# Key reads of an attention kernel shared by two issuing engines: lower partition quarters from SP, upper quarters from ACT

## The chip, the cores and the metric

The kernel runs on one core of one Trainium2 chip. The metric is the time of one execution on the device in microseconds (us). A core has a matrix engine (PE), three engines for elementwise work (DVE, ACT, POOL) and SP, which here only issues transfers. 16 DMA engines move data between device memory and the on-chip memory, which has 128 partitions.

## What is computed

Three layers over 8 sequences of 64 rows by 512, with a context of 8 x 1601 x 512, all in f32. Cut to what matters:

```python
def _L0_xattn_ref(q, k, v, Wq, bq, Wk, bk, Wv, bv):
    qp = q @ Wq + bq;  kp = k @ Wk + bk;  vp = v @ Wv + bv
    attn = softmax(qp @ kp.T / sqrt(512))
    return attn @ vp
...
x = x + _L0_xattn_ref(_layernorm(x), ctx_1024, ctx_1024, ...)
x = x + _L0_attn_ref(_layernorm(x), ...)      # 16 heads, sigmoid gates, no softmax
x = x + _L0_ffn_ref(_layernorm(x), ...)       # each row to one of 8 experts
return x
```

## The kernel before

The 8 sequences are worked in four pairs (p = 0 to 3; k = 0, 1 is the member of a pair). Pair 0 is written out, pairs 1 and 2 are the two passes of a loop, pair 3 is written out again, and the experts follow. The key projection is folded into the queries, so the scores are products of queries with the raw context rows. For that the rows are wanted twice: as they are (CTX, for the weighted sums) and turned (CT, for the scores).

**Two ways to turn.** The 1601 keys are 13 tiles of 128, two tiles to a group (groups 0 to 6). In some groups PE turns the tiles of CTX and ACT (k = 0) and DVE (k = 1) copy them into CT (`turn_keys`, `move_keys`). The others are "split" groups (1, 2, 3 in pair 0; 1 to 5 later): `load_split` reads them a second time from device memory straight into FF, in four partition quarters of 32 (`quad`), each quarter taking 128 of the 512 columns in runs of 512 bytes, and DVE turns them in 32x32 blocks by two STREAM_TRANSPOSE (`turn_split`, L847), no PE needed. A part of `SPLIT_PARTS` is what one wait covers: (1, 2), (3), (4), (5). Each part takes 8 transfers (4 quarters x 2 members): 256 KB each for the part of two groups, 128 KB each for one group. Only when all 8 have landed may DVE start on a group of the part. FF has three slots for groups, so 4 and 5 reuse those of 1 and 2, and a part may be read once the group that held its slot has been turned (semaphore `keysT_made`).

**Order of the work.** Every engine works through its own program in order. In a pair p, PE runs 14 half groups of scores (u = 0 to 13); between them stand the steps of the second layer for pair p-1 (L1169 to L1376). Then the scores' softmax is made (DVE maxima, ACT exponentials L686), PE turns the numerators (L1261), ACT and DVE move them (L347), and PE makes the weighted sums with CTX (L1290) in four chunks c = 0 to 3. Here ACT also makes 16 small copies of the next pair's queries (L678), and DVE, at c = 1, turns the next pair's groups 1 and 2. Behind these four transposes DVE has the last numerators (c = 3), the routing steps L975 to L995 of pair p-1 and the reciprocal of the softmax sums (L895). ACT's L693 needs this reciprocal, and PE's first transposes of the next pair's second-layer steps (L1169, A<-sq) need L693.

**Who issues.** SP issues all reads of the context: in `next_split` the next pair's part 1 (group 3) and part 0 (groups 1 and 2), in `load_pair` CTX chunks 0 and 1, then parts 2 and 3 (groups 4 and 5) and CTX chunks 3 and 2. ACT issues none. In pair 0's prologue SP issues parts 0 and 1 while PE and ACT make the queries (ACT L661, L667).

Of the kernel before, what the change touches and what calls it, by code (L numbers as in the profile page):

```python
# [8 lines left out]
P = 128  # L9
# [8 lines left out]
QUADS = P // Q  # L18
BLOCKS = GT * P // Q
SLOT_OF = {1: 0, 2: 1, 3: 2, 4: 0, 5: 1}  # L20
SPLIT_PARTS = ((1, 2), (3,), (4,), (5,))
EARLY = 2
TURN_FIRST = 6
CHUNKS = [(0, 4), (4, 8), (8, FULL), (FULL, KT)]
NCH = len(CHUNKS)

# [89 lines left out]
def program(nc, A):  # L116
# [4 lines left out]
    with ctx:  # L121
# [181 lines left out]
        def settle(eng):  # L303

            eng.sem_inc(s["passed"], 1)
# [17 lines left out]
        def split_turned(p, n):  # L323

            return 2 * n if is_first(p) else 2 * len(NEXT.split) * p + 2 * (len(FIRST.split) - len(NEXT.split) + n)
# [5 lines left out]
        def move_keys(eng, copy, p, k, t):  # L331

            if t is None:
                return
            o = order_of(p)
            pos, w = o.at[t // GT], P if t < FULL else TAIL
            eng.wait_ge(s[f"turned{k}"], keys_moved(p, o.tiles.index(t) + 1))

            slot_free(eng, p, pos)
            copy(ctxT[:, pos % 2, k, :, (t % GT) * P:(t % GT) * P + w], turned_bank(TR[k])[:, :, 0:w]).then_inc(s[f"moved{k}"], 1)  # L340

        def move_numerators(eng, copy, p, c):

            lo, hi = CHUNKS[c]
            w = P if c < NCH - 1 else TAIL
            eng.wait_ge(s[f"turned{c % 2}"], numerators_moved(p, c // 2 + 1))
            copy(probs[0:w, lo:hi, :], TR[c % 2][0:w, 0:(hi - lo) * P].rearrange("p (t q) -> p t q", q=P)).then_inc(s[f"moved{c % 2}"], 1)  # L347

        @block.sync  # L350
        def _(sp):
            def load_ctx(b, k, c):
# [8 lines left out]
            def load_split(p, part):

                first, slot = SPLIT_PARTS[part][0] * GT * P, SLOT_OF[SPLIT_PARTS[part][0]]
                n = len(SPLIT_PARTS[part]) * BLOCKS
                for quad in range(QUADS):
                    for k in range(2):
                        src = A["ctx"][bass.ds(2 * p + k, 1), first:first + n * Q, quad * P:(quad + 1) * P]
                        sp.dma_start(split[quad * Q:(quad + 1) * Q, k, slot * BLOCKS:slot * BLOCKS + n, :],
                                     src.rearrange("a (b r) d -> r (a b) d", r=Q)).then_inc(s_split[part], 16)

            def next_split(p):

                if is_first(p):
                    sp.wait_ge(s["keysT_made"], split_turned(0, 2))
                    load_split(1, 0)
                    sp.wait_ge(s["keysT_made"], split_turned(0, 3))
                    load_split(1, 1)
                    return
                sp.wait_ge(s["keysT_made"], split_turned(p, order_of(p).split.index(3) + 1))
                settle(sp)  # L380
                load_split(p + 1, 1)
                sp.wait_ge(s["keysT_made"], split_turned(p, len(order_of(p).split)))
                settle(sp)
                load_split(p + 1, 0)

            def load_chunk(p, c):

# [6 lines left out]
            def load_pair(p):  # L394

                load_chunk(p, 0)
                load_chunk(p, 1)
                sp.wait_ge(s["keysT_made"], split_turned(p, 2))
                settle(sp)
                load_split(p, 2)  # L400
                load_split(p, 3)
                load_chunk(p, 3)
                load_chunk(p, 2)

# [22 lines left out]
            load_x(0)  # L427
            for c in (0, 2, 3):
                load_chunk(0, c)
            load_split(0, 0)  # L430
            load_split(0, 1)

            sp.wait_ge(s["qp_made"], 2 * DC)
            load_weight(awq, "awq", "aq_in")
# [205 lines left out]
        def _(act):  # L640
# [9 lines left out]
            for half in range(2):  # L650
                if half == 0:
                    move_x0(0)
                    move_x0(1)
                    act.wait_ge(s["vec_in"], 16)

                for m in range(DC):
                    if half == 0 and m == DC - 1:
                        move_x0(2)
                        move_x0(3)
                    act.wait_ge(s["qp_made"], DC * half + m + 1)  # L660
                    a.activation(qpT[:, m, 2 * P * half:2 * P * (half + 1)], AB[m % 2][:, 0:2 * P], ACT.Identity,  # L661
                                 bias=vec[:, 0, m:m + 1]).then_inc(s["qp_moved"], 1)

            def move_qk(first, m):
                n = slice(0, P) if first else slice(P, PAIRS * P)
                act.wait_ge(s["qk_made"], (m if first else DC + m) + 1)
                a.copy(qk[:, m, n], AB[m % 2][:, n]).then_inc(s["qk_moved"], 1)  # L667

            for m in range(DC):
                move_qk(True, m)  # L670

            def next_queries(p, last, chunks=range(DC)):

                act.wait_ge(s["qk_moved"], 2 * DC)
                act.wait_ge(s["scored"], GROUPS * (p - 1) + last)
                for m in chunks:
                    for j in range(QUADS):
                        a.copy(qcurP[m * Q:(m + 1) * Q, j, :], qk[j * Q:(j + 1) * Q, m, bass.ds(p * P, P)]).then_inc(s["qcurP_made"], 1)  # L678
# [10 lines left out]
            def attention(p, step):  # L689
# [49 lines left out]
                elif step == "route":  # L739
                    act.wait_ge(s["top_made"], p + 1)  # L740
                    act.wait_ge(s["pow3"], p + 1)
                    a.activation(sm[:, 2:3], sm[:, 0:1], ACT.Exp, scale=rstd[:, 3:4]).then_inc(s["en_made"], 1)

            for t in FIRST.tiles[:GT]:
                move_keys(act, a.copy, 0, 0, t)
            move_qk(False, 0)
            move_qk(False, 1)
            for t in FIRST.tiles[GT:]:
                move_keys(act, a.copy, 0, 0, t)
            act.wait_ge(s["c_made"], 1)  # L750
            a.copy(call[:], AB[1][:, 0:PAIRS + E]).then_inc(s["c_moved"], 1)
            exponentials(0)
# [796 lines left out]
```

## Time and profile before

| | |
|---|---|
| median of 3 runs | 333.71 us (331.84 to 335.01) |
| the profiled execution | 333.99 us, of which the span of the trace is 332.3 us |
| PE busy | 301.6 us (91%) |
| DVE, ACT, POOL busy | 161.2, 90.7, 78.4 us |
| TensorE's granted clock, mean | 0.996 of full speed |
| moved by the 16 DMA engines | 74.27 MB, 224 GB/s over the span |
| reads of FF from the context | 80 of 128 KB and 32 of 256 KB, all issued by SP |

The page of the profile gives shares; the views of the trace give single waits and times. In a timeline a row is the start, the length, the engine, the line of the kernel and the operation with its tiles (written<-read), and in square brackets how long the engine stood idle before it and what ended that. SPq and ACTq are the instruction streams (sequencers) of SP and ACT: a DMA_DIRECT2D there is the issue of a transfer, not the transfer.

### The profile page before, as it was taken

How to read it: one execution, taken by the hardware profiler on the slowest of the kernel's cores; microseconds unless marked ns; L12 is line 12 of the kernel's file. 1: busy time of each engine (PE TensorE's matmuls, PEld its weight loads, DVE VectorE, ACT ScalarE, POOL GpSimd, SP SyncE). 2: the span in 40 equal slices, each digit the busy share in tenths (PEclk: the TensorE clock that was granted, in tenths of full speed). 3: DMA queues.
4: the chain of work that ended last, by engine and by line, in shares of the span. 5: the costliest groups of instructions: out<-in, count | busy, mean ns of one | idle time of the engine just before them, and what ended most of it. 6: DMA issues, size and time to landing. Idle time of an engine off the chain costs nothing. (4 is left out here: it accounts for less than half of the span.)

```text
span 332.3 us, 5209 instructions
## 1 busy us (share of the span) xinstructions
PE 301.6 (91%) x1806; PEld 159.8 (48%) x1806; DVE 161.2 (49%) x364; ACT 90.7 (27%) x209; POOL 78.4 (24%) x84
## 2 busy tenths in 40 slices
PE   0999899999899889999989999999998989899792
PEld 0788567643454544445455445455543344443330
DVE  3303338537263763828185833738561354735431
ACT  1132230235112346321234442124411013411110
POOL 5000003167022500112340020135102246103202
PEclk9999999999999999999999999999999999999998
DMA  7999999999999998999949699952715996153300
GB/s 250 390 374 172 184 311 387 211 187 257 387 211 228 279 187 132 375 250 227 324 77 192 116 393 220 258 204 83 298 63 145 396 411 266 28 205 109 119 2 34
DMA packets 61364, 74.27 MB, mean 224 GB/s; under 512 B 3187, under 2 KB 40083, under 8 KB 60320
## 3 DMA queue, kind: packets, MB, share of 16 engines
q1 hardware_dynamic: 59792, 69.23, 80.2%
q0 software_dynamic: 1552, 4.78, 4.0%
q8 instruction: 12, 0.20, 0.3%
q14 instruction: 8, 0.07, 0.1%
HBM read 70.85 MB, written 3.67 MB: 224 GB/s over the span
## 5 line engine op out<-in xcount | busy, mean ns | idle before, releaser
L1251 PE MATMUL SC<-CT_sb,QC_sb 128*64 128x256 f32 x384 | 50.4, 389 | 0.3 <-DVE CT_sb L847 0.2
L847 DVE STREAM_TRANSPOSE CT_sb<-FF_sb 128x1024 f32<-128x1024 f32 x36 | 42.4, 1220 | 14.3 <-DMA FF_sb<-ctx 12.7
L1290 PE MATMUL ST<-CTX_sb,PR_sb 128*64 128x512 f32 (+1 forms) x208 | 48.2, 600 | 1.1 <-ACT PR_sb L347 1.1
L1251 PEld LDWEIGHTS SC<-CT_sb,QC_sb 128*64 128x64 f32 x384 | 24.7, 136 | 17.2 <-issue 9.0
L1176 PE MATMUL A<-AW_sb,normT_sb 128*128 128x512 f32 x64 | 29.4, 599 | 1.3 <-DVE normT_sb L918 1.3
L1290 PEld LDWEIGHTS ST<-CTX_sb,PR_sb 128*64 128x64 f32 (+1 forms) x208 | 13.9, 136 | 23.2 <-issue 22.3
L532 POOL TENSOR_TENSOR rn_sb<-ss_sb,nhalf_sb 128x16 f32<-128x16 f32 x4 | 11.7, 2915 | 33.9 <-DVE ss_sb L923 33.9
L1176 PEld LDWEIGHTS A<-AW_sb,normT_sb 128*128 128x128 f32 x64 | 11.7, 190 | 14.8 <-issue 12.2
L1169 PE MATMUL TR<-ident_sb,CTX_sb 128*128 128x128 f32 (+1 forms) x128 | 16.1, 266 | 2.3 <-DVE CT_sb L340 1.1
L1196 PE MATMUL A<-AW_sb,WQK_sb 128*128 128x256 f32 x64 | 16.4, 422 | 0.8 <-ACT AW_sb L645 0.8
L1169 PEld LDWEIGHTS TR<-ident_sb,CTX_sb 128*128 128x128 f32 (+1 forms) x128 | 12.9, 141 | 8.7 <-issue 5.6
L340 DVE COPY CT_sb<-TR 128x512 f32<-128x512 f32 (+1 forms) x16 | 10.0, 625 | 13.2 <-PE TR L1169 13.0
L340 ACT COPY CT_sb<-TR 128x512 f32<-128x512 f32 (+1 forms) x16 | 8.6, 535 | 25.6 <-PE TR L1169 25.5
L1176 PE MATMUL A<-AO_sb,rawT_sb 128*128 128x512 f32 x32 | 14.8, 605 | 0.7 <-DVE rawT_sb L962 0.6
L1176 PE MATMUL A<-WV_sb,rawT_sb 128*128 128x512 f32 x32 | 14.8, 605 | 0.7 <-ACT rawT_sb L696 0.7
L1196 PEld LDWEIGHTS A<-AW_sb,WQK_sb 128*128 128x128 f32 x64 | 13.6, 215 | 3.3 <-issue 1.1
L1219 PE MATMUL A<-AO_sb,WQK_sb 128*128 128x128 f32 (+1 forms) x64 | 14.6, 383 | 0.7 <-ACT AO_sb L661 0.7
L678 ACT COPY QC_sb<-QK_sb 32x128 f32 (+1 forms) x48 | 14.2, 295 | 1.1
L900 DVE TENSOR_TENSOR x_sb<-A,xrow_sb 128x512 f32<-128x512 f32 x4 | 2.8, 692 | 23.0 <-PE A L1176 23.0
L535 POOL TENSOR_TENSOR rn_sb<-ss_sb,nhalf_sb 128x16 f32<-128x16 f32 x4 | 11.6, 2903 | 7.5 <-DVE ss_sb L930 7.5
L855 DVE COPY QC_sb<-QK_sb 32x128 f32<-32x128 f32 x16 | 3.9, 241 | 18.5 <-ACT QK_sb L667 18.0
L526 POOL TENSOR_TENSOR rstd_sb<-rstd_sb,halves_sb 128x3 f32<-128x3 f32 x4 | 3.5, 872 | 38.3 <-DVE rstd_sb L908 38.3
(227 smaller groups left out, 459.0 us busy)
## 6 DMA issues: line engine op xcount, KB each, us to landing
CTX_sb<-ctx SPq DMA_DIRECT2D x24, 1024.0 KB, 10.7
FF_sb<-ctx SPq DMA_DIRECT2D x80, 128.0 KB, 7.2
FF_sb<-ctx SPq DMA_DIRECT2D x32, 256.0 KB, 7.9
CTX_sb<-wgu SPq DMA_DIRECT2D x4, 1024.0 KB, 9.4
CTX_sb<-wdn SPq DMA_DIRECT2D x5, 512.0 KB, 12.8
FF_sb<-wgu SPq DMA_DIRECT2D x2, 1024.0 KB, 6.6
rows<-XR_sb SPq DMA_DIRECT2D x3, 512.0 KB, 10.7
CTX_sb<-ctx SPq DMA_DIRECT2D x8, 130.0 KB
```

Source lines behind the costliest of these rows:

```text
L340: copy(ctxT[:, pos % 2, k, :, (t % GT) * P:(t % GT) * P + w], turned_bank(TR[k])[:, :, 0:w]).then_inc(s[f"moved{k}"], 1)
L532: g.tensor_tensor(rn[:, 0:HEADS], ss[:, 0:HEADS], nhalf[:, 0:HEADS], ALU.pow).then_inc(s["powq"], 1)
L535: g.tensor_tensor(rn[:, HEADS:], ss[:, HEADS:], nhalf[:, HEADS:], ALU.pow).then_inc(s["powk"], 1)
L678: a.copy(qcurP[m * Q:(m + 1) * Q, j, :], qk[j * Q:(j + 1) * Q, m, bass.ds(p * P, P)]).then_inc(s["qcurP_made"], 1)
L847: v.transpose(ctxT[:, pos % 2, k, :, :].rearrange("p c (b r) -> p b c r", r=Q), split[:, k, at:at + BLOCKS, :].rearrange("p b (c r) -> p b ...
L855: v.tensor_copy(qcurP[m * Q:(m + 1) * Q, j, :], qk[j * Q:(j + 1) * Q, m, 0:P]).then_inc(s["qcurP_made"], 1)
L1169: last = t_.transpose(bank[:, c * w:c * w + n], rows[:, c * P:(c + 1) * P], ident[0:n, 0:n])
L1176: last = t_.matmul(bank, left[:, c, :], right[:, c, :], start=(c == 0), stop=(c == DC - 1))
L1196: last = t_.matmul(AB[m % 2][:, 0:2 * P], wq[:, c, m * P:(m + 1) * P], xnT[:, c, 2 * P * half:2 * P * (half + 1)], start=(c == 0), stop=(c ...
L1219: last = t_.matmul(AB[m % 2][:, n], wkT[:, c, m * P:(m + 1) * P], qpT[:, c, n], start=(c == 0), stop=(c == DC - 1))
L1251: last = t_.matmul(out[q, :], (qcurP if split_group else qcur)[:, c, q], ctxT[:, pos % 2, k, c, 0:n], start=(c == 0), stop=(c == DC - 1))
L1290: last = t_.matmul(ST[q, :], probs[0:w, t, q], ctxb[0:w, k, t, :], start=(t == 0), stop=(t == KT - 1))
```

## The change

`load_split` becomes a helper with an engine and a list of quarters. SP keeps the quarters 0 and 1 (partitions 0 to 63, `LOWER`, 4 transfers a part), ACT gets the quarters 2 and 3 (`UPPER`). Groups 4 and 5 become one part of 8 transfers of 256 KB (before: two parts, 16 of 128 KB). Over the kernel 112 transfers, all from SP, become 88, 44 from each. ACT's issues stand in its program at these places: in the prologue one after each of the last four L661 and one after each of the first four L667; in pair 0 after its last key copy and after the first numerators; in pairs 1 to 3 part 2 after u = 1; in pairs 1 and 2 the next pair's part 1 after u = 5 and part 0 after the first numerators.

```diff
-SPLIT_PARTS = ((1, 2), (3,), (4,), (5,))
+SPLIT_PARTS = ((1, 2), (3,), (4, 5))
+LOWER, UPPER = ([(quad, k) for quad in range(lo, lo + QUADS // 2) for k in range(2)] for lo in (0, QUADS // 2))
+UPPER_REST, UPPER_FIRST = 1, 5
...
+        def load_split(eng, p, part, quads):
...
+            for quad, k in quads:
+                src = A["ctx"][bass.ds(2 * p + k, 1), first:first + n * Q, quad * P:(quad + 1) * P]
+                eng.dma_start(split[quad * Q:(quad + 1) * Q, k, slot * BLOCKS:slot * BLOCKS + n, :],
...
-                load_split(p, 2)
-                load_split(p, 3)
+                load_split(sp, p, 2, LOWER)
...
+                    if half == 1:
+                        load_split(act, 0, 0, UPPER[m:m + 1])
...
                 move_qk(True, m)
+                load_split(act, 0, 1, UPPER[m:m + 1])
...
+            def upper_first(p, n, part):
+                act.wait_ge(s["keysT_made"], split_turned(p, n))
...
+                load_split(act, p + 1, part, UPPER)
+            def upper_rest(p):
+                act.wait_ge(s["keysT_made"], split_turned(p, 2))
...
                     move_keys(act, a.copy, p, 0, NEXT.tile(u))
+                    if u == UPPER_REST:
+                        upper_rest(p)
+                    if u == UPPER_FIRST and not is_last(p):
+                        upper_first(p, NEXT.split.index(3) + 1, 1)
                 exponentials(p)
                 for step in by_max:
                     attention(p - 1, step)
                 move_numerators(act, a.copy, p, 0)
+                if not is_last(p):
+                    upper_first(p, len(NEXT.split), 0)
```

ACT's program in the loop, from the softmax's exponentials (PR<-SC) on, before. An ISA or REGISTER_ALU row is register work for the instruction behind it.

```order
L686 ACTIVATE PR_sb,esum_sb<-SC,mx_sb 128x512 x2
L686 ACTIVATE PR_sb,esum_sb<-ST,mx_sb 128x65
L346 REGISTER_ALU
L347 COPY PR_sb<-TR 128x512 [waits turned0]
L675 REGISTER_ALU [waits qk_moved]
L678 ISA [waits scored]
L678 COPY QC_sb<-QK_sb 32x128
```

The same place of the changed kernel (its L349 is L347 of before):

```order
L690 ACTIVATE PR_sb,esum_sb<-SC,mx_sb 128x512 x2
L690 ACTIVATE PR_sb,esum_sb<-ST,mx_sb 128x65
L348 REGISTER_ALU
L349 COPY PR_sb<-TR 128x512 [waits turned0]
L750 REGISTER_ALU
L358 ISA [waits keysT_made]
L358 DMA FF_sb<-ctx 32x16x128
L358 ISA
L358 DMA FF_sb<-ctx 32x16x128
L358 ISA
L358 DMA FF_sb<-ctx 32x16x128
```

Four issues for the next pair's groups 1 and 2 now stand between the numerators' copy and the query copies.

ACT's program in pair 0's prologue, where it moves the projected queries out of PSUM (AO<-A, then QK<-A), before:

```order
L661 ACTIVATE AO_sb<-A,vec_sb 128x256 [waits qp_made] x2
L645 COPY AW_sb<-TR 128x4x128 [waits xnT_turned] x2
L661 ACTIVATE AO_sb<-A,vec_sb 128x256 [waits qp_made] x5
L667 COPY QK_sb<-A 128x128 [waits qk_made] x4
L340 COPY CT_sb<-TR 128x4x128 [waits turned0] x2
```

and changed:

```order
L662 ACTIVATE AO_sb<-A,vec_sb 128x256 [waits qp_made]
L358 DMA FF_sb<-ctx 32x16x128
L662 ACTIVATE AO_sb<-A,vec_sb 128x256 [waits qp_made]
L358 DMA FF_sb<-ctx 32x16x128
L670 COPY QK_sb<-A 128x128 [waits qk_made]
L358 DMA FF_sb<-ctx 32x8x128
L670 COPY QK_sb<-A 128x128 [waits qk_made]
L358 DMA FF_sb<-ctx 32x8x128
```

Behind each of eight moves there is now an issue that stands ahead of the next move.

SP's program from the reads of pair 1's groups 1 and 2 (32x16x128) and group 3 (32x8x128) to pair 1's first CTX chunk, before:

```order
L368 DMA FF_sb<-ctx 32x16x128 [waits keysT_made]
L368 DMA FF_sb<-ctx 32x16x128 x7
L368 DMA FF_sb<-ctx 32x8x128 [waits keysT_made]
L368 DMA FF_sb<-ctx 32x8x128 x7
L406 DMA AO_sb<-awo 128x4x512 [waits c_made,qk_made]
L356 DMA CTX_sb<-ctx 128x4x512 [waits pv_chunk]
```

and changed:

```order
L358 DMA FF_sb<-ctx 32x16x128 [waits keysT_made]
L358 DMA FF_sb<-ctx 32x16x128 x3
L358 DMA FF_sb<-ctx 32x8x128 [waits keysT_made]
L358 DMA FF_sb<-ctx 32x8x128 x3
L407 DMA AO_sb<-awo 128x4x512 [waits c_made,qk_made]
L368 DMA CTX_sb<-ctx 128x4x512 [waits pv_chunk]
```

SP comes to the CTX chunk after 8 issues in place of 16.

## Rows read from the trace of the kernel before

**Rows 1.** The page, busy time, share of the span and instructions.
```profile
PE 301.6 (91%) x1806; PEld 159.8 (48%) x1806; DVE 161.2 (49%) x364; ACT 90.7 (27%) x209; POOL 78.4 (24%) x84
```

**Rows 2.** Waits: who waited for whom, us in total, times, longest.
```profile
PE TR L1169 <- DMA CTX_sb<-ctx: 1.0, 1, 1.0
DVE CT_sb L847 <- DMA FF_sb<-ctx: 12.7, 4, 5.4
```

**Rows 3.** Stretches of pair 1 and pair 2: length, busy per engine, clock, DMA, GB/s.
```profile
81.80:140.60 58.80, 54.83 (x335) 27.90 (x331) 31.76 (x67) 19.24 (x46) 10.04 (x8) 1.00 1.06 259
140.60:197.70 57.10, 54.68 (x335) 28.08 (x335) 32.43 (x69) 19.23 (x46) 11.97 (x11) 1.00 0.98 222
```

**Rows 4.** Timeline of PE: start, length, work, idle before and its end.
```profile
89.45 0.66 PE L1169 MATMUL TR<-ident_sb,CTX_sb 128*128 128x128 f32 x4 [0.95 <-DMA CTX_sb<-ctx]
...
117.88 0.63 PE L1169 MATMUL A<-ident_sb,kh_sb 128*128 128x128 f32 x4 [1.14 <-DVE res_sb L945]
...
142.03 0.66 PE L1169 MATMUL A<-ident_sb,sq_sb 128*128 128x128 f32 x4 [0.39 <-ACT sq_sb L693]
...
198.72 0.66 PE L1169 MATMUL A<-ident_sb,sq_sb 128*128 128x128 f32 x4
```

**Rows 5.** Timeline of DVE, the block transposes that stood waiting in pairs 1 and 2.
```profile
102.45 2.37 DVE L847 STREAM_TRANSPOSE CT_sb<-FF_sb 128x1024 f32<-128x1024 f32 x2 [5.40 <-DMA FF_sb<-ctx]
...
132.43 4.63 DVE L847 STREAM_TRANSPOSE CT_sb<-FF_sb 128x1024 f32<-128x1024 f32 x4 [4.31 <-DMA FF_sb<-ctx]
...
186.38 4.63 DVE L847 STREAM_TRANSPOSE CT_sb<-FF_sb 128x1024 f32<-128x1024 f32 x4 [1.17 <-DMA FF_sb<-ctx]
```

**Rows 6.** Timeline of ACT around the places where issues are put.
```profile
28.10 0.47 ACT L661 ACTIVATE AO_sb<-A,vec_sb 128x256 f32<-128x256 f32 x1 [1.25 <-PE A L1196]
...
30.78 0.27 ACT L667 COPY QK_sb<-A 128x128 f32<-128x128 f32 x1 [0.63 <-PE A L1219]
...
88.61 0.59 ACT L340 COPY CT_sb<-TR 128x512 f32<-128x512 f32 x1 [4.57 <-PE TR L1169]
...
125.88 0.59 ACT L347 COPY PR_sb<-TR 128x512 f32<-128x512 f32 x1 [0.20 <-PE TR L1261]
126.37 2.54 ACT L678 COPY QC_sb<-QK_sb 32x128 f32 x8
131.43 0.59 ACT L738 COPY normT_sb<-A 128x512 f32<-128x512 f32 x1 [2.53 <-PE A L1169]
...
137.90 2.53 ACT L678 COPY QC_sb<-QK_sb 32x128 f32 x8
...
182.98 0.59 ACT L347 COPY PR_sb<-TR 128x512 f32<-128x512 f32 x1 [0.20 <-PE TR L1261]
```

**Rows 7.** Timeline of SP's issues.
```profile
16.90 22.03 SPq L368 DMA_DIRECT2D FF_sb<-ctx  x16
...
75.63 1.15 SPq L356 DMA_DIRECT2D CTX_sb<-ctx  x1
...
130.61 0.38 SPq L356 DMA_DIRECT2D CTX_sb<-ctx  x1
...
172.94 6.09 SPq L368 DMA_DIRECT2D FF_sb<-ctx  x8
...
187.71 0.96 SPq L356 DMA_DIRECT2D CTX_sb<-ctx  x2
```

**Rows 8.** Line L368 in 172 to 180 us: issue in ns, min/median/max.
```profile
L368 SPq DMA_DIRECT2D FF_sb<-ctx x8: 316/348/1477, 172.9 to 177.8; - x8
```

**Rows 9.** Stretches with FF reads alone, then CTX reads alone; columns as rows 3.
```profile
178.00:182.00 4.00, 3.80 (x24) 1.99 (x25) 2.04 (x6) 1.63 (x5) 0.00 (x0) 1.00 1.25 184
...
190.00:194.00 4.00, 4.00 (x25) 1.83 (x23) 2.03 (x6) 0.36 (x2) 0.00 (x0) 1.00 1.04 400
```

**Rows 10.** DMA in 114 to 122 us, 40 slices of 0.2 us, FF reads.
```profile
GB/s 151 164 172 179 177 184 177 161 197 200 197 169 192 202 220 151 141 159 164 225 220 228 207 151 167 166 179 264 228 197 143 146 282 202 187 192 154 143 141 164
```

**Rows 11.** Line L776, the end of ACT's loop, in 138 to 140 us.
```profile
L776 ACTq COMPARE_BRANCH  x1: 45/45/45, 138.9 to 138.9; - x1
```

More of the change, by code:

```diff
@@ L347, in move_numerators @@
             copy(probs[0:w, lo:hi, :], TR[c % 2][0:w, 0:(hi - lo) * P].rearrange("p (t q) -> p t q", q=P)).then_inc(s[f"moved{c % 2}"], 1)
+        def load_split(eng, p, part, quads):
+            first, slot = SPLIT_PARTS[part][0] * GT * P, SLOT_OF[SPLIT_PARTS[part][0]]
+            n = len(SPLIT_PARTS[part]) * BLOCKS
+            for quad, k in quads:
+                src = A["ctx"][bass.ds(2 * p + k, 1), first:first + n * Q, quad * P:(quad + 1) * P]
+                eng.dma_start(split[quad * Q:(quad + 1) * Q, k, slot * BLOCKS:slot * BLOCKS + n, :],
+                              src.rearrange("a (b r) d -> r (a b) d", r=Q)).then_inc(s_split[part], 16)
         @block.sync
@@ L359, in load_ctx @@
                     sp.dma_start(ctxb[0:TAIL, k, FULL, :], src).then_inc(s_ctx[k][c], 16)
[L361 to L369, printed above, removed]
             def next_split(p):
@@ L374, in next_split @@
                     sp.wait_ge(s["keysT_made"], split_turned(0, 2))
-                    load_split(1, 0)
+                    load_split(sp, 1, 0, LOWER)
                     sp.wait_ge(s["keysT_made"], split_turned(0, 3))
-                    load_split(1, 1)
+                    load_split(sp, 1, 1, LOWER)
                     return
@@ L380, in next_split @@
                 settle(sp)
-                load_split(p + 1, 1)
+                load_split(sp, p + 1, 1, LOWER)
                 sp.wait_ge(s["keysT_made"], split_turned(p, len(order_of(p).split)))
                 settle(sp)
-                load_split(p + 1, 0)
+                load_split(sp, p + 1, 0, LOWER)
             def load_chunk(p, c):
@@ L429, in _ @@
                 load_chunk(0, c)
-            load_split(0, 0)
-            load_split(0, 1)
+            load_split(sp, 0, 0, LOWER)
+            load_split(sp, 0, 1, LOWER)
             sp.wait_ge(s["qp_made"], 2 * DC)
@@ L742, in attention @@
                     a.activation(sm[:, 2:3], sm[:, 0:1], ACT.Exp, scale=rstd[:, 3:4]).then_inc(s["en_made"], 1)
+            def upper_first(p, n, part):
+                act.wait_ge(s["keysT_made"], split_turned(p, n))
+                if not isinstance(p, int):
+                    settle(act)
+                load_split(act, p + 1, part, UPPER)
+            def upper_rest(p):
+                act.wait_ge(s["keysT_made"], split_turned(p, 2))
+                settle(act)
+                load_split(act, p, 2, UPPER)
             for t in FIRST.tiles[:GT]:
@@ L749, in _ @@
                 move_keys(act, a.copy, 0, 0, t)
+            upper_first(0, 2, 0)
             act.wait_ge(s["c_made"], 1)
@@ L756, in _ @@
                 move_numerators(act, a.copy, 0, c)
+                if c == 0:
+                    upper_first(0, 3, 1)
             next_queries(1, FIRST.at[FIRST.split[-1]] + 1)
```

## The prediction

> **What bounds the kernel now.** I read the page first: PE is busy for 91% of the span, no other engine for half of it [rows 1]. The clock is full, so PE's own work sets the time, and a change of reads can only move what PE stands idle for. Next the waits: only one wait of PE names a transfer, 1.0 us. DVE waited 12.7 us in four times for the split reads in FF [rows 2], so the question is how much of DVE's lateness comes through to PE. For that I set pairs 1 and 2 side by side, since both are passes of the same loop. Pair 1 took 58.80 us, pair 2 57.10, with the same 335 matmuls and nearly the same PE busy time [rows 3]. The surplus of 1.7 us is what late reads cost PE. The timeline shows where. At 89.45 PE waits 0.95 us for a CTX chunk. At 117.88 it waits 1.14 us for a DVE product that was late because DVE had waited 5.40 us for group 4 at 102.45 [rows 4, 5]; to this I put the other 0.75 us of the surplus. The rest of the waits for FF reached PE hardly at all. So a perfect supply of reads is worth 1.7 us, plus 0.39 us at 142.03 (below). That is 0.6% of the time, and no faster transfer can give more while PE has its work to do.
>
> **The gain.** SP has 8 issues fewer ahead of pair 1's first CTX chunk, which it sent at 75.63 [rows 7]. At 0.35 us each [rows 8] these are 2.8 us, so the wait of 0.95 us goes. For the other 0.75 us group 4 must land by about 101.5 in place of 102.45. It now comes in one part with group 5, 2 MB where DVE waited for 1 MB, sent by both engines from about 83. Eight such reads took 13.4 us in pair 2 (below), and the tail of four CTX chunks is ahead of them: 97 to 101. I take the whole 1.7 us, and 0.95 as the lower bound.
>
> **ACT's issues, where they cost nothing.** An issue of 256 KB into a queue with room took SP 316 to 348 ns (median), up to 1477 once the queue was full [rows 8]. With the register work of the loop in between I count 0.55 us each on ACT, 2.2 us for four, 0.35 to 0.5 us each in the unrolled prologue. In the prologue ACT stands idle 1.25 us before each L661 and 0.63 us before each L667 [rows 6], which covers the eight issues. After u = 1 there are 4.57 us free before 88.61. After the first numerators, the query copies end 2.2 us later, at 131.1 in place of 128.9, and the next move, at 131.43, is not touched [rows 6]. Uncovered, the 44 issues at 0.5 us would be 22 us, so the cover matters (second rival).
>
> **The loss.** This is what the order of ACT shows. Groups 1 and 2 of the next pair are a part that DVE needs whole. SP still sends its half as soon as group 5 is turned (in pair 2 at 172.94 [rows 7]). ACT sends the other half only behind the exponentials and the first numerators. In pair 2 that is 10 us behind SP's half.
>
> How long does this half take? In pair 2 of before, eight reads (2.10 MB) sent from 172.94 [rows 7] had landed when DVE started at 186.38 [rows 5]: 13.4 us. At the 184 GB/s that FF reads reach [rows 9] the data take 11.4 us, so 2.0 us are the way in and out. Four reads (1.05 MB) then take 5.7 + 2.0 = 7.7 us, alone in the engines. They land at 133.7 and 190.8. But SP sends CTX chunks at 130.61 and 187.71 [rows 7], which meet the last 1.1 us or so of the data. Shared evenly this adds 1.1 us (134.8, 191.9), and if CTX gets two turns of three, 2.2 us (135.9, 193.0). I take the middle of the first two, 134.3 and 191.4, since nothing shows how two queues share.
>
> When must they be there? In pair 1 DVE started at 132.43, and PE's step 9.6 us later at 142.03 already waited 0.39 us for the chain behind it (four transposes 4.63 us, numerators, routing, reciprocal, L693) [rows 4, 5]. So there is no slack: the loss is 134.3 - 132.43 = 1.9 us (1.3 to 3.5). In pair 2 the same step began at 198.72 without a wait. 9.6 us ahead of it is 189.1, which DVE's 186.38 met with 2.7 us to spare. The loss is 191.4 - 189.1 = 2.3 us (1.7 to 3.9). Pair 0's reads for pair 1 go from both engines at 57 us and are early. Parts 1 and (4, 5) have many microseconds left in every pair, and after pair 3's scores nothing is changed.
>
> A rule of the Trainium skill bears on the rate: *SBUF — State Buffer*, section "Door 1: The DMA port swizzle", says that partitions 0 to 63 reach only 8 of 16 ports and 64 to 127 the other 8, with 196 GB/s measured for 64 partitions. The trace agrees: 184 GB/s for quarters against 400 for all partitions [rows 9]. Its next section says that two transfers to the two halves do not add up. Slices of 264 and 282 GB/s stand where the reads go from quarter to quarter [rows 10], which speaks for some adding up. By either the late half lands alone, so the sum stays.
>
> **Sum.** -1.7 + 1.9 + 2.3 = +2.5 us on the profiled execution of 333.99 us, 336.5. The median of the runs shown lies 0.3 us below that execution: **336.2 us**, 0.7% above the median of before. With the bounds of the two losses (3.0 to 7.4) and a gain from 0.95 to 1.7 it is 335.0 to 340.2.
>
> **Rivals.**
> *The late half does no harm (0.20).* If four reads, alone, run well above 184 GB/s or the copies' sequencer lets them go earlier, both losses shrink. At 400 GB/s [rows 9] they take 2.6 + 2.0 us and land at 130.6 and 187.7, ahead of 132.43 and 189.1. Only the gain is left, and at best the 0.39 us with it: 331.6 to 332.0. For it: the peaks [rows 10]. Against: 184 GB/s was held over 4 us [rows 9].
> *ACT's issues are held up by SP's (0.27).* In the prologue, with its queue full, SP took 22.03 us for 16 issues, 1.4 us each [rows 7]. If ACT must wait while SP's issue is stuck, its issue costs 1.4 us more. Each of four moves then comes 1.4 + 0.5 - 1.25 = 0.6 us late, and of four more 1.4 + 0.35 - 0.63 = 1.1 us, with PE waiting for each of them: up to 6.8 us, half of it if SP is through early. After u = 1 in pair 1, where SP's queue is full again, four issues take 8 us against 4.57 [rows 6], 3 us more. This decides from 1.3 us an issue on, and gives 336.2 + 3 to 10 = 339 to 346, about 342. Against it: ACT's queue itself is empty.
> *Perfetto Trace Analysis* in the Trainium skill, section "DMA Instruction — HWDGE (DVE, Sync)", says that the descriptor generator is locked for one issue at a time; no run here shows a second issuing engine, so it is this rival's rule and not the forecast's.
> *It is faster by over 1% (0.04).* It needs 3.3 us and PE's waits for reads hold 2.1. It would take some other stall that transfers cause inside busy time, and pairs 1 and 2 have the same busy time at 259 and 222 GB/s [rows 3].
>
> **How the numbers follow.** The forecast has 0.47, its own range 335.0 to 339.0. The rest, 0.02, is for what I don't see. About 1% is what a measurement of this kernel can tell from no change: below 330.4 is faster, above 337.0 slower. Of the forecast's 0.47 I put a quarter above 337.0, and all of the second rival: 0.12 + 0.27 = 0.39 slower. Faster 0.05, the same 0.56. The range for 8 in 10 goes from 331.8 to 342.0: it leaves out the upper half of the second rival and the lowest edge of the first.
>
> **What would show it.** Right: in pairs 1 and 2 DVE's transposes of the next pair's groups 1 and 2 wait longer for FF (start near 134 and 191, counted as above), PE waits for L693 about 2 us in each, PE no longer waits at a CTX turn in pair 1, and ACT's issues take 0.3 to 0.5 us. The pairs would take about 57.1 + 1.9 and 57.1 + 2.3, with the wait at the end of one counted in the next. Wrong: ACT's issues of over a microsecond and PE waiting for L661 and L667 in the first 35 us (second rival), or DVE starting at its old times (first). Group 4 landing later than 103 in pair 1 would make the gain's second half wrong.

## The result and the profile after

The changed kernel takes 347.62 us (median of 4 runs, 345.06 to 349.03) against 332.92 us for the kernel before (4 runs, 331.84 to 335.01): a ratio of 1.042, 95% interval 1.034 to 1.051. It is 14.7 us slower. The forecast was 336.2 us, range 331.8 to 342.0, with 0.39 for slower. The forecast lies 11.4 us too low, and the time is outside the range. Ratios, here and below, leave out the few executions in a slower state of the chip.

The profiled execution took 345.06 us with a span of 343.3 us, 11.0 us more than before. First the page, busy time and then the granted clock in 40 slices:

```profile
PE 304.0 (89%) x1806; PEld 160.5 (47%) x1806; DVE 162.2 (47%) x364; ACT 91.0 (26%) x209; POOL 78.7 (23%) x84
...
PEclk9999999999999999699999999999999999999998
```

PE does the same 1806 matmuls [rows 1]. Its busy time grew by 2.4 us, and one slice shows a lower clock; the other 8.6 us are idle. This execution is the fastest of the four. The other three, with mean clocks of 0.968 to 0.981 against its 0.987, took 1.9 to 4.0 us longer, so the 14.7 us between the medians hold more of a low clock than this trace shows. Who waits for whom, us in total, times and longest:

```profile
DVE CT_sb L873 <- DMA FF_sb<-ctx: 32.8, 5, 8.1
...
PE A L1195 <- DVE res_sb L971: 3.2, 3, 1.1
PE A L1366 <- issue: 2.4, 2, 1.2
PE A L1397 <- DVE onehot_sb L1008: 2.1, 2, 1.7
PE A L1195 <- DVE qh_sb L952: 2.0, 2, 1.4
```

DVE's waits for the split reads went from 12.7 to 32.8 us [rows 2], and PE now waits for DVE's products in several places. The timeline of DVE tells which reads are late, start, length, work and the idle time before it:

```profile
99.98 2.37 DVE L873 STREAM_TRANSPOSE CT_sb<-FF_sb 128x1024 f32<-128x1024 f32 x2 [5.15 <-DMA FF_sb<-ctx]
132.77 4.62 DVE L873 STREAM_TRANSPOSE CT_sb<-FF_sb 128x1024 f32<-128x1024 f32 x4 [7.12 <-DMA FF_sb<-ctx]
164.48 2.37 DVE L873 STREAM_TRANSPOSE CT_sb<-FF_sb 128x1024 f32<-128x1024 f32 x2 [6.68 <-DMA FF_sb<-ctx]
195.86 4.62 DVE L873 STREAM_TRANSPOSE CT_sb<-FF_sb 128x1024 f32<-128x1024 f32 x4 [5.72 <-DMA FF_sb<-ctx]
227.31 2.37 DVE L873 STREAM_TRANSPOSE CT_sb<-FF_sb 128x1024 f32<-128x1024 f32 x2 [8.11 <-DMA FF_sb<-ctx]
```

A row x2 is group 4, a row x4 the next pair's groups 1 and 2. Before, group 4 was waited for in pair 1 alone [rows 5]. Now it is late in pairs 2 and 3 too, which the forecast did not have.

Where the 11.0 us arise is read from PE, the same work in both kernels. From the timeline of before, four rows beside those of [rows 4]:

```profile
82.76 0.66 PE L1169 MATMUL A<-ident_sb,sq_sb 128*128 128x128 f32 x4
...
149.15 1.09 PE L1169 MATMUL TR<-ident_sb,CTX_sb 128*128 128x128 f32 x8
...
196.78 1.08 PE L1290 MATMUL ST<-CTX_sb,PR_sb 65*64 65x512 f32 x4
...
234.52 0.69 PE L1251 MATMUL ST<-CT_sb,QC_sb 128*64 128x65 f32 x16
```

and after:

```profile
81.72 0.66 PE L1195 MATMUL A<-ident_sb,sq_sb 128*128 128x128 f32 x4
...
115.42 0.63 PE L1195 MATMUL A<-ident_sb,kh_sb 128*128 128x128 f32 x4 [0.96 <-DVE res_sb L971]
...
138.87 0.18 PE L1397 MATMUL A<-onehot_sb,before_sb 128*128 128x8 f16 x1 [1.74 <-DVE onehot_sb L1008]
...
140.90 1.98 PE L1277 MATMUL SC<-CT_sb,QC_sb 128*64 128x256 f32 x8 [0.81 <-ACT QC_sb L682]
142.81 1.12 PE L1195 MATMUL A<-ident_sb,sq_sb 128*128 128x128 f32 x4
...
151.81 1.09 PE L1195 MATMUL TR<-ident_sb,CTX_sb 128*128 128x128 f32 x8
...
202.10 1.08 PE L1316 MATMUL ST<-CTX_sb,PR_sb 65*64 65x512 f32 x4
...
206.12 0.66 PE L1195 MATMUL A<-ident_sb,sq_sb 128*128 128x128 f32 x4 [1.08 <-ACT sq_sb L697]
...
245.59 0.69 PE L1277 MATMUL ST<-CT_sb,QC_sb 128*64 128x65 f32 x16
```

| the same work, before and after | offset | arose since the last row |
|---|---|---|
| 82.76, 81.72 (pair 1's first layer-2 step) | -1.0 | -1.0: not by the change, see below |
| 117.88, 115.42 (pair 1, middle) | -2.5 | -1.4: the gain |
| 142.03, 142.81 (pair 2's first layer-2 step) | +0.8 | +3.2: groups 1 and 2 late |
| 149.15, 151.81 | +2.7 | +1.9: the clock |
| 196.78, 202.10 (end of pair 2's sums) | +5.3 | +2.7: group 4 late in pair 2 |
| 198.72, 206.12 | +7.4 | +2.1: groups 1 and 2 late |
| 234.52, 245.59 (end of pair 3's scores) | +11.1 | +3.7: group 4 late in pair 3 |

So groups 1 and 2 cost 3.2 + 1.9 + 2.1 = 7.2 us, groups 4 and 5 cost 6.4 us, and 2.5 us came back. The first 1.0 us of these stood already in the prologue, ahead of ACT's first issue at 21.97, as the same move of ACT shows, before and after:

```profile
21.20 0.47 ACT L661 ACTIVATE AO_sb<-A,vec_sb 128x256 f32<-128x256 f32 x1 [1.09 <-PE A L1196]
...
20.23 0.47 ACT L662 ACTIVATE AO_sb<-A,vec_sb 128x256 f32<-128x256 f32 x1 [1.09 <-PE A L1222]
```

From trace to trace of the later experiments too PE comes to pair 1 at different times, 81.7 to 84.3 where the clock stays full, so pairs are compared below by their own lengths.

The clock is seen in the stretches (length, busy time of PE, PEld, DVE, ACT, POOL, granted clock, DMA share, GB/s):

```profile
139.00:145.00 6.00, 5.19 (x24) 2.47 (x24) 1.80 (x8) 2.92 (x8) 2.36 (x4) 0.59 1.15 279
145.00:155.00 10.00, 10.00 (x54) 5.29 (x52) 4.22 (x11) 1.17 (x2) 1.33 (x2) 0.91 1.15 228
```

A mean of 0.59 lies near the lower of TensorE's two levels, 1.2 GHz. Behind the waits of 1.74 and 0.81 us, eight score products take 1.98 us where 1.08 is usual.

### Why group 4 is late

SP's issues before, from the reads of groups 4 and 5 in pair 2 to CTX chunks 3 and 2:

```profile
137.29 13.31 SPq L368 DMA_DIRECT2D FF_sb<-ctx  x16
151.31 0.85 SPq L359 DMA_DIRECT2D CTX_sb<-ctx  x2
```

after, SP and then ACT:

```profile
140.07 1.24 SPq L358 DMA_DIRECT2D FF_sb<-ctx  x1
141.63 2.87 SPq L371 DMA_DIRECT2D CTX_sb<-ctx  x2
144.74 0.97 SPq L368 DMA_DIRECT2D CTX_sb<-ctx  x2
...
144.27 2.07 ACTq L358 DMA_DIRECT2D FF_sb<-ctx  x4
```

Before, the CTX chunks stood behind the split reads in one queue, and the first of them was issued at 151.31, behind the last read. Now SP is done with its half by 141.3 and sends the chunks, while ACT's half goes out from 144.27 in a queue of its own. The DMA queues in 150 to 156 us of after, packets, MB, share of 16 engines (q1 is SP's, q10 ACT's):

```profile
q1 hardware_dynamic: 678, 1.35, 82.4%
q10 hardware_dynamic: 666, 0.33, 26.9%
```

Before, the eight reads issued in 137 to 144 us had 7.3/8.1/8.4.

The Trainium skill, *DMA: Bandwidth & Descriptors*, section "Queues, rings and completion order", says that each engine takes turns between queues packet by packet. The trace agrees: 678 against 666.

### The profile page after: what moved, and what is told of

Read it like the earlier page. It is cut to its first block and busy times, and to the rows that moved or that the text cites. A ratio compares the mean times of both kernels' runs of the same rounds, so it can differ in the third digit from the quotient of the medians.

```text
span 343.3 us, 5166 instructions
## 1 busy us (share of the span) xinstructions
PE 304.0 (89%) x1806; PEld 160.5 (47%) x1806; DVE 162.2 (47%) x364; ACT 91.0 (26%) x209; POOL 78.7 (23%) x84
## 5 line engine op out<-in xcount | busy, mean ns | idle before, releaser
L873 DVE STREAM_TRANSPOSE CT_sb<-FF_sb 128x1024 f32<-128x1024 f32 x36 | 42.4, 1220 | 34.4 <-DMA FF_sb<-ctx 32.8
L1277 PE MATMUL SC<-CT_sb,QC_sb 128*64 128x256 f32 x384 | 52.3, 400 | 1.8 <-ACT QC_sb L682 0.8
L1222 PE MATMUL A<-AW_sb,WQK_sb 128*128 128x256 f32 x64 | 15.7, 409 | 0.8 <-ACT AW_sb L646 0.8
L1245 PE MATMUL A<-AO_sb,WQK_sb 128*128 128x128 f32 (+1 forms) x64 | 14.6, 384 | 0.7 <-ACT AO_sb L662 0.7
L1222 PEld LDWEIGHTS A<-AW_sb,WQK_sb 128*128 128x128 f32 x64 | 13.1, 208 | 3.1 <-issue 1.1
## 6 DMA issues: line engine op xcount, KB each, us to landing
CTX_sb<-wdn SPq DMA_DIRECT2D x5, 512.0 KB, 12.8
```

What stands on the lines that cost most here:

```text
L873: v.transpose(ctxT[:, pos % 2, k, :, :].rearrange("p c (b r) -> p b c r", r=Q), split[:, k, at:at + BLOCKS, :].rearrange("p b (c r) -> p b ...
L1222: last = t_.matmul(AB[m % 2][:, 0:2 * P], wq[:, c, m * P:(m + 1) * P], xnT[:, c, 2 * P * half:2 * P * (half + 1)], start=(c == 0), stop=(c ...
L1245: last = t_.matmul(AB[m % 2][:, n], wkT[:, c, m * P:(m + 1) * P], qpT[:, c, n], start=(c == 0), stop=(c == DC - 1))
L1277: last = t_.matmul(out[q, :], (qcurP if split_group else qcur)[:, c, q], ctxT[:, pos % 2, k, c, 0:n], start=(c == 0), stop=(c == DC - 1))
```

## The experiments

Two theories from the traces. **Place:** ACT's halves of groups 1 and 2 go out behind exponentials and numerators, 8 to 10 us after SP's halves. **Sharing:** the halves of groups 4 and 5 lie beside the CTX chunks in place of ahead of them. Rivals: a second queue costs as such; ACT's issues are held up by SP's; the merge of groups 4 and 5 costs by itself. All times are medians, ratios against the kernel before on the same chip. "Less" below is against the changed kernel's 347.62 us, which was measured apart from these runs. The kernel before had medians of 332.92, 333.41, 333.39 and 333.92 us in the four groups of measurements, so a difference of 1 us between groups says nothing.

| kernel | edit against | us | ratio, 95% |
|---|---|---|---|
| a_rest_sp | changed: part (4, 5) all from SP | 340.81 | 1.018 to 1.029 |
| b_first_sp | changed: groups 1, 2 of pairs 2, 3 all from SP | 340.77 | 1.019 to 1.034 |
| c_both_sp | changed: a and b | 334.54 | 0.999 to 1.007 |
| e_held | changed: CTX chunks held back | 340.87 | 1.017 to 1.028 |
| f_early | changed: ACT's issues for 1, 2 earlier | 340.32 | 1.017 to 1.030 |
| i_early_held | changed: e and f | 332.03 | 0.993 to 0.9998 |
| g_early_rest_sp | changed: f and a | 333.70 | 0.997 to 1.003 |
| h_unmerged | changed: groups 4, 5 as two parts | 340.49 | 1.008 to 1.024 |
| k_unmerged_early_held | changed: e, f and h | 333.16 | 0.996 to 1.001 |
| d_merge | before: groups 4, 5 as one part | 339.54 | 1.015 to 1.026 |
| j_fill | changed: PE kept busy in a wait | 347.45 | 1.038 to 1.050 |

### Taking one half back to SP

```diff
-                load_split(sp, p, 2, LOWER)
+                load_split(sp, p, 2, LOWER + UPPER)
...
-                    if u == UPPER_REST:
-                        upper_rest(p)
```

> The changed kernel, but SP issues all eight reads of groups 4 and 5 again (still one part); ACT keeps the upper halves of the other parts. Theory Q (queue sharing): in the changed kernel ACT's half of groups 4 and 5 takes turns, packet by packet, with the 2 MB of the CTX chunk that SP sent ahead of it or beside it, lands 7 to 8 us later than DVE wants it, and PE loses 2.7 us in pair 2 and 3.7 us in pair 3, plus some of the time at a lower clock. Then this run gains 6 to 9 us on the changed kernel: 339 to 341, and DVE's transposes of group 4 stand no longer than in the kernel before. Rival U (a second issuing engine as such costs, by whatever way): 12 of 44 issues fewer give 12/44 of 14.7 us, so 343 to 344. Rival M (one part for groups 4 and 5 is the cause): no gain, 347.

340.81 us, 6.8 less, as expected. DVE waits for group 4 in pair 1 alone (5.45 us), and for groups 1 and 2 as in the changed kernel (7.12 and 6.05 us).

```diff
-                load_split(sp, p + 1, 0, LOWER)
+                load_split(sp, p + 1, 0, LOWER + UPPER)
...
-                if not is_last(p):
-                    upper_first(p, len(NEXT.split), 0)
```

> The changed kernel, but for pairs 2 and 3 SP issues all eight reads of groups 1 and 2; ACT keeps the rest. Theory P (place in ACT's program): ACT sends its half only behind the first numerators, 8 to 10 us after SP; it costs PE 2.8 us in pair 1 and 2.4 us in pair 2, and the idle time ahead of the dip of the granted clock around 139 us. Then this run gains 5 to 8 us: 339.5 to 342.5, and the clock has no dip there. Rival U: 8 of 44 issues fewer, 345. Rival M: 347.

340.77 us, 6.85 less, as expected. The waits for groups 1 and 2 go to 1.59 and 1.42 us, those for group 4 stay (9.30 and 7.70 us in pairs 2 and 3), and the clock stays at 1.00 from 130 to 150 us.

> Both of the former: ACT issues only for pair 0, for pair 1's groups 1 to 3 and the upper halves of group 3. Theories P and Q together: no late reads are left, the early CTX chunk of pair 1 stays, 331.5 to 333. Rival U: 24 of 44 issues are left on ACT, so half of the loss, 340. Rival M: 347, or at least well above 335.

Both edits: 334.54 us, 13.1 less. The two losses add up, and are 7 us each by the medians (what of this is the clock is said below). The 331.5 to 333 that was expected is missed by 1.5 us. ACT still issues 24 reads here (pair 0's, pair 1's groups 1 and 2, and group 3's), and the time is 0.3% above the kernel before, not told from none, so a second issuing engine as such costs 2 us at most (the interval ends at 1.007).

### Mending the order and leaving the issues on ACT

```diff
                 load_split(sp, p, 2, LOWER)
+                sp.wait_ge(s_split[2], 16 * 2 * QUADS * p)
+                settle(sp)
                 load_chunk(p, 3)
```

> The changed kernel with one wait more: SP sends the CTX chunks 3 and 2 only when the eight reads of groups 4 and 5 have landed. ACT's issues, their places and the merged part are as in the changed kernel. Theory Q: ACT's half has the engines to itself and SP's half, lands within 8 us of its issue, so group 4 is in time: 339 to 341 as with these reads on SP. Rival U and rival M: 347 or slower, since a wait is added and nothing taken away.

340.87 us, 6.75 less, with every one of the 44 issues still on ACT. Only the time at which SP sends the CTX chunks (and what stands behind them in its program) changed, so without the sharing group 4 is not late. Whether the sharing alone makes it late is asked below. DVE's wait for it in pair 1 is 1.38 us.

```diff
+                if not is_last(p):
+                    upper_first(p, len(NEXT.split), 0)
                 exponentials(p)
                 for step in by_max:
                     attention(p - 1, step)
                 move_numerators(act, a.copy, p, 0)
-                if not is_last(p):
-                    upper_first(p, len(NEXT.split), 0)
```

> The changed kernel with ACT's four issues for the next pair's groups 1 and 2 moved ahead of its exponentials (all groups have been turned by then, and ACT stands idle there 3.9 us). Nothing else moves, the number of issues and of queues stays. Theory P (the place in ACT's program makes the half late): DVE finds groups 1 and 2 landed or nearly so, PE's 1.7 us wait for the one-hot rows in pair 1 and the clock's dip behind it go: 339.5 to 342.5, as with these reads on SP, and groups 4 still late. Rival U (the second queue as such): 347.

340.32 us, 7.3 less. The waits for groups 1 and 2 are 1.57 and 1.31 us: the place in ACT's program was the cause.

> Both mends at once, all 44 issues still on ACT: groups 1 and 2 sent ahead of the exponentials, CTX chunks 3 and 2 held until groups 4 and 5 have landed. Theories P and Q together: no read is late, and pair 1's CTX wait stays away: 331.5 to 334, at best 0.4% below the kernel before. Rival U: clearly above 335.

Both: **332.03 us** (10 runs, 331.02 to 333.95), 15.6 less than the changed kernel and 0.4% below the kernel before; the interval, 0.993 to 0.9998, only just leaves out no change. Its DVE timeline:

```profile
96.98 2.37 DVE L875 STREAM_TRANSPOSE CT_sb<-FF_sb 128x1024 f32<-128x1024 f32 x2 [1.23 <-DMA FF_sb<-ctx]
127.55 4.62 DVE L875 STREAM_TRANSPOSE CT_sb<-FF_sb 128x1024 f32<-128x1024 f32 x4 [1.73 <-DMA FF_sb<-ctx]
155.98 2.37 DVE L875 STREAM_TRANSPOSE CT_sb<-FF_sb 128x1024 f32<-128x1024 f32 x2 [3.14 <-DMA FF_sb<-ctx]
184.17 4.62 DVE L875 STREAM_TRANSPOSE CT_sb<-FF_sb 128x1024 f32<-128x1024 f32 x4 [1.26 <-DMA FF_sb<-ctx]
210.51 2.37 DVE L875 STREAM_TRANSPOSE CT_sb<-FF_sb 128x1024 f32<-128x1024 f32 x2 [1.01 <-DMA FF_sb<-ctx]
```

Of that hardly anything reaches PE: the 0.41 us at 139.73 below was 0.39 us before. Pairs 1 and 2 in its timeline of PE:

```profile
82.64 0.66 PE L1197 MATMUL A<-ident_sb,sq_sb 128*128 128x128 f32 x4
...
139.73 0.66 PE L1197 MATMUL A<-ident_sb,sq_sb 128*128 128x128 f32 x4 [0.41 <-ACT sq_sb L699]
...
196.41 0.66 PE L1197 MATMUL A<-ident_sb,sq_sb 128*128 128x128 f32 x4
```

Pair 1 takes 57.1 us where it was 59.3 (82.76 above to 142.03 [rows 4]), pair 2 takes 56.7 as before.

> The changed kernel with ACT's issues for groups 1 and 2 ahead of the exponentials and the merged part (4, 5) all from SP. Theory (place in ACT's program, queue sharing): both losses go, since the halves of groups 1 and 2 are sent in time and the CTX chunks stand behind the part (4, 5) in one queue again. It should come to the kernel that has both all on SP (334.5 us): 333 to 336 us, with DVE waiting for FF at most about 5 us in pair 1 (group 4, behind a full queue). If a second queue as such costs something: 338 us or more.

333.70 us, the time of the kernel before (333.92 on that chip). DVE waits 5.01 us for group 4 in pair 1, yet pair 1 takes 57.7 us (84.28 to 141.97), 1.6 us less than before. The gain is there, and is lost ahead of it: PE comes to pair 1 1.5 us later than before, 0.6 us of it already ahead of ACT's first issue and 0.9 us by ACT's issues in the prologue (see "ACT's issues" below).

### The merge of groups 4 and 5

```diff
-SPLIT_PARTS = ((1, 2), (3,), (4, 5))
+SPLIT_PARTS = ((1, 2), (3,), (4,), (5,))
...
                 load_split(sp, p, 2, LOWER)
+                load_split(sp, p, 3, LOWER)
...
                 load_split(act, p, 2, UPPER)
+                load_split(act, p, 3, UPPER)
```

> The changed kernel with groups 4 and 5 as two parts again, each split between SP and ACT (8 issues of 128 KB on either engine after u = 1). It tells how much of the lateness of groups 4 and 5 (about 6.4 us of the 14.7 us lost) comes from DVE having to wait for both groups at once, and how much from ACT's half sharing the DMA engines packet for packet with SP's CTX chunks. If it is the merge: group 4's upper half is half the data, lands some 5 us sooner than the 14.4 us of the changed kernel, DVE does not wait for it, and the time is 341 to 343 us. If it is the sharing: group 4 is better but group 5 is as late as before, the time is 344 to 347 us. If eight issues in a row hold up ACT's key copies: over 347 us.

340.49 us, 7.1 less, 0.5 us below the 341 to 343 that was expected if the merge matters. No wait of DVE for group 4 or 5 is left in its trace: two waits, 12.8 us, both for groups 1 and 2. So it takes both, the sharing and the merge, to make group 4 late in pairs 2 and 3: with the merge but the chunks behind the reads again (a_rest_sp, e_held) it is in time, and with the sharing but without the merge it is too. Either edit removes the same 7 us, so the 7 us can't be divided between them.

> The changed kernel with all three mended: ACT's issues for groups 1 and 2 ahead of the exponentials, SP waiting for the FF reads of groups 4 and 5 before it sends CTX chunks 3 and 2, and groups 4 and 5 as two parts. The kernel with the first two mended took 332.0 us and DVE still waited 1.2 to 3.1 us for group 4 in each pair. If those waits still reach PE, 330 to 331.5 us; if PE has no wait left that they cause, 332 us as before; if the eight issues in a row on ACT cost more than that, 333 us or more.

333.16 us (12 runs). The unmerged parts remove DVE's last waits for group 4, and PE gains nothing by it: pairs 1 and 2 take 57.1 and 56.7 us (83.62 to 140.70 to 197.37), as in i_early_held. The median is 1.1 us above that of i_early_held, measured on another chip; against its own kernel before it is 0.2% faster, not told from none. It lies where eight issues in a row were expected to cost something, but the trace doesn't show them as the cause: the 1.0 us between the two profiled executions is there when PE comes to pair 1 (83.62 against 82.64), ahead of the first of them.

```diff
-SPLIT_PARTS = ((1, 2), (3,), (4,), (5,))
+SPLIT_PARTS = ((1, 2), (3,), (4, 5))
...
                 load_split(p, 2)
-                load_split(p, 3)
```

> The kernel before with the one part of the change that needs no ACT: groups 4 and 5 as one part of eight 256 KB reads, all from SP. Theories P and Q: group 4 then waits for 2 MB in place of 1 MB, but all of it is ahead of the CTX chunks in one queue; DVE waits some 3 us in each pair and has 4 us to spare: 332 to 335, the same as before. Rival M (the merge is what costs): 340 or more.

339.54 us, 6 more than before, where 332 to 335 was expected: a miss, just under the 340 of the rival. A part is seen in the timeline of DVE, and of PE behind it:

```profile
106.68 2.37 DVE L846 STREAM_TRANSPOSE CT_sb<-FF_sb 128x1024 f32<-128x1024 f32 x2 [8.91 <-DMA FF_sb<-ctx]
```

```profile
110.60 0.63 PE L1168 MATMUL A<-ident_sb,kh_sb 128*128 128x128 f32 x4 [1.81 <-ACT sq_sb L711]
113.60 0.66 PE L1168 MATMUL A<-ident_sb,qh_sb 128*128 128x128 f32 x4 [1.35 <-DVE qh_sb L925]
116.49 1.08 PE L1339 MATMUL A<-WQK_sb,rawT_sb 128*64 128x256 f32 x8 [1.22 <-issue]
```

In pair 1 the part stands behind SP's full queue, and DVE needs 2 MB of it in place of 1. Pair 1 takes 61.6 us (84.66 to 146.25) against 59.3. So the merge by itself costs 2.3 us when SP sends everything, which neither theory had. Another 3 us or so is a fall of the clock in pair 0 (columns as above):

```profile
56.00:60.00 4.00, 4.00 (x21) 2.84 (x22) 3.08 (x5) 0.00 (x0) 0.00 (x0) 0.50 1.06 376
60.00:64.00 4.00, 4.00 (x32) 2.92 (x30) 0.00 (x0) 0.17 (x1) 0.19 (x1) 0.85 1.22 179
```

No wait of PE over 0.2 us stands in the 16 us ahead of it, and all four runs of this kernel have a mean clock of 0.985 to 0.987. e_held shows the same fall at the same place, while before and the changed kernel run the same products there at the full clock. Why it comes there, and whether the merge has a part in it, is open.

### The clock

```diff
                 elif step == "rank":
+                    if not is_last(p):
+                        for _ in range(12):
+                            t_.matmul(A1[:, P:2 * P], ident[:], ident[:], start=True, stop=True)
                     pe.wait_ge(s["hot_made"], p + 1)
```

> The changed kernel with 12 idle-filling 128x128 products (some 1.6 us of PE) ahead of PE's wait for the one-hot rows in pairs 1 and 2; they write a bank that holds nothing. In the changed kernel PE stood there 1.74 us in pair 1 and 0.33 us in pair 2, and behind pair 1's wait the granted clock was 0.59 for 6 us and 0.91 for 10 us. If the idle time brings the lower clock down, the clock stays at 1.0 there and the run gains 2.8 us and loses at most 1.3 us in pair 2: 345 to 347 against 347.6, with a mean clock of 0.995 or more. If the dip has another cause, the clock stays near 0.987 and the time is 348 to 349.

The 12 products take 2.94 us where PE waited 1.74, and in the stretch the clock stays full:

```profile
137.25 2.94 PE L1397 MATMUL A<-ident_sb 128*128 128x128 f32 x24
...
142.51 0.66 PE L1195 MATMUL A<-ident_sb,sq_sb 128*128 128x128 f32 x4 [0.39 <-ACT sq_sb L697]
```

```profile
139.00:145.00 6.00, 5.61 (x39) 3.21 (x39) 1.69 (x9) 3.04 (x8) 2.16 (x4) 1.00 1.14 285
```

All four runs have mean clocks of 0.995 to 0.997, the changed kernel's 0.968 to 0.987. So PE's idle time is what brought the clock down here. The median is 347.45 us, unchanged, where 345 to 347 was expected. The products stand at three places and not at two, as the expectation has it, and take 8.8 us, where PE had waited 2.1. At the end of pair 3's scores this execution is still 1.1 us ahead of the changed kernel's (244.53 against 245.59); the third set, at 255.20, where PE did not wait, takes 2.9 us more. By the offsets the clock took 1.9 us, and 0.9 more in the slower products ahead of 142.81. That is read from one execution, and the medians don't settle its size.

The clock is also in the 7 us that each mend was worth. Mean clocks are 0.968 to 0.987 in the changed kernel, 0.983 to 0.987 in a_rest_sp and e_held, and 0.991 to 0.998 in b_first_sp and f_early but for one run of 0.977. Within h_unmerged alone 337.68 us stand at 0.997, and 340.42 and 340.57 us at 0.987 and 0.985. Between the profiled executions a_rest_sp is 4.8 us faster than the changed kernel, b_first_sp 5.5, c_both_sp 10.5, e_held 4.2 (with the fall in pair 0, 3 us, against it) and f_early 5.9. So both causes stand and add up either way, but each is 7 us by the medians and 4 to 6 us by these.

## Why the prediction was wrong

**What bounds the kernel: right.** PE's work is the bound, and a supply in time is worth about 2 us: i_early_held, where late reads hardly reach PE, gained 2.2 us in pair 1, and nothing in pair 2.

**The gain: right in size, wrongly taken apart.** PE no longer waits at the CTX turn, and from 82.76 (after: 81.72) to 117.88 (115.42) pair 1 gained 1.4 us of the 1.7 forecast. But the 0.95 us of that wait and the 0.75 us at 117.88 were not two gains. PE's step at 117.88 begins 15.43 us behind DVE's start on group 4 at 102.45; after it is 15.44 us (99.98 to 115.42), in d_merge 15.43 (106.68 to 122.11). While group 4 is that late, its landing alone sets this step: an earlier CTX chunk would only have made PE wait longer there, so the 0.95 us were no lower bound, and the whole 1.7 us asked for group 4 at 100.75, not at 101.5. Counted from the start of the pair it came 1.4 us sooner than before, and that is the gain. In i_early_held, with group 4 at 96.98, PE's wait at this step is down to 0.21 us, and the whole 2.2 us are gained ahead of it.

**ACT's issues: right for this trace, not for all.** 44 of them took 317/384/2072 ns (min/median/max), near the 0.32 to 0.35 of SP. In the prologue, beside SP's full queue, the four of 256 KB took 0.32 to 0.39 us each and the four of 128 KB 0.44 to 1.05, all under the 1.3 us from which the rival in which SP's stuck issues hold up ACT's decides. The longest held the next query move up by 0.2 us, and from the first of the L1245 products to pair 1 PE took 53.96 us (27.76 to 81.72) against 54.04 before (28.72 to 82.76). Other traces of the same prologue show some of what this rival said. In g_early_rest_sp the first issue of 128 KB took 1.82 us, ACT's moves came late behind it and the next ones, and PE waited for them (before: 0.24 and 1.08 us in this place):

```profile
30.53 1.82 ACTq L358 DMA_DIRECT2D FF_sb<-ctx  x1
...
36.38 1.19 PE L1193 MATMUL TR<-ident_sb,CTX_sb 128*128 128x128 f32 x8 [1.63 <-ACT CT_sb L342]
```

The same stretch took 54.92 us there, and 54.34 to 54.50 in c_both_sp, k_unmerged_early_held and h_unmerged, whose longest issues took 1.32 to 1.48 us. So this rival is worth 0 to 0.9 us in place of its 3 to 10, and whether SP's stuck issue or ACT's own filling queue holds an issue up is open. The time fell into the rival's range for another reason.

```profile
L358 ACTq DMA_DIRECT2D FF_sb<-ctx x44: 317/384/2072, 22.0 to 208.3; - x44
```

**The late half of groups 1 and 2: right mechanism, too small.** ACT issued at 123.69 and 188.19, right behind the start of the numerators' copy, as the forecast had it, and the half landed 9.1 and 7.7 us later (forecast: 8.3, with 7.7 alone). The loss in pair 2 is 2.1 us (forecast 2.3). In pair 1 it is 3.2 us and 1.9 behind it (forecast 1.9, at most 3.5). 0.8 us is the later landing. The rest is a term that was missing from the sum: behind PE's waits of 1.74 and 0.81 us the clock stood at 0.59 for 6 us. The runs b_first_sp and f_early put the whole at 6.9 and 7.3 us, forecast 4.2; the clock is in these too.

**The step that failed** is one sentence: "Parts 1 and (4, 5) have many microseconds left in every pair". True for part 1; for (4, 5) it costs 6.4 us in the trace, and 6.75 to 7.1 us by the medians of three experiments. Two things that the diff showed were left out. The priority that SP's one queue gave the reads over CTX chunks 3 and 2 was lost, and DVE had to wait for 2 MB in place of 1, which was reckoned with in pair 1 alone. The sharing of two queues was asked for the four reads of groups 1 and 2 and the first chunks, as 1.1 us, and not for group 4, where the four transfers of CTX chunks 3 and 2, in packets of 2 KB, stand against it. At 0.33 MB in 6 us, ACT's 1 MB takes 19 us, and the last of it did land 18.4 us after its issue. With this term of about 6.5 and the clock's 3 the sum of +2.5 is +12. Between the two profiled executions (345.06 and 333.99) it was 11.1, and 12.1 without the 1.0 us that the changed kernel's was ahead by chance when it came to pair 1. The 14.7 of the medians is 3.6 more: the changed kernel's profiled execution lies 2.6 below its median, that of the kernel before 1.1 above.

**The rates: right.** Two engines reading into disjoint halves did not add up. In i_early_held, with both halves under way in 143 to 151 us and the engines full, the queues carried

```profile
DMA packets 2987, 1.49 MB, mean 186 GB/s; under 512 B 94, under 2 KB 2984, under 8 KB 2987
...
q10 hardware_dynamic: 1562, 0.78, 63.3%
q1 hardware_dynamic: 1425, 0.71, 61.8%
```

186 GB/s, where one queue had 184 [rows 9]. The Trainium skill, *SBUF — State Buffer*, section "Can I just issue two DMAs to hit both halves?", says so, and the peaks of 264 and 282 [rows 10], which I had taken for some adding up, did not come to more over a stretch of 8 us.

**The chances.** The sum's bounds gave 335.0 to 340.2, but the chance of 0.47 was put on 335.0 to 339.0 without a reason. It changes nothing here: the time lies above both, and the range's top of 342.0 came from a rival that was worth 0.9 us at most.

## What to carry to other kernels

Transfers in one queue have an order, and a tuned kernel may live by it: before half of them goes to a second queue, list what stood behind them and will now run beside them, with the packet size of each, since the engines share by packets and not by bytes. An issue put into a compute engine's program goes out when that engine comes to it, so place it by the time at which its slot comes free. If the split is wanted, hold the less urgent transfers back by a wait on the urgent ones: here that was worth 6.75 us by the medians, and with the earlier issues it turned a loss of 4.2% into a gain of 0.4%, itself at the edge of what the runs can tell.

## What the runs showed of the hardware that I had not expected

- Packet for packet sharing of SP's and ACT's queues: 678 against 666 packets, 1.35 against 0.33 MB, in 6 us.
- Two queues filling disjoint halves of the partitions together carried 186 GB/s, one carried 184.
- An issue on ACT starts while the copy ahead of it still runs: L349's copy runs from 123.42 for 0.59 us, the first issue starts at 123.69.
- ACT's issues of 128 KB in the prologue, beside SP's full queue, took 0.44 to 1.05 us in one trace and 0.86 to 1.82 in another (g_early_rest_sp), where PE lost 0.9 us by them.
- Ahead of anything that the change does, the same move of ACT began at 20.23 us in one trace and at 21.20 in another, and PE came to pair 1 1.0 us apart. Why is open.
- PE's granted clock fell to about 0.5 in two stretches that no visible wait of PE leads into (d_merge and e_held, pair 0). What brings it down there is open.
